# Second cross attention: the value sums of two quads take turns in PSUM banks 2 and 7

## The reference, cut to what matters

```python
def _L1_xattn_ref(query, key, value, mask, Wq, bq, Wk, bk, Wv, bv, Wo, bo):
    ...
    q = proj(query, Wq, bq)
    k = proj(key, Wk, bk)
    v = proj(value, Wv, bv)
    scale = 1.0 / jnp.sqrt(jnp.asarray(DK, q.dtype))
    score = jnp.einsum('bhqd,bhkd->bhqk', q, k) * scale
    m = mask[:, None, :, :]
    score = jnp.where(m == 0, jnp.asarray(-1000000000.0, score.dtype), score)
    p = jax.nn.softmax(score, axis=-1)
    x = jnp.einsum('bhqk,bhkd->bhqd', p, v)
    x = x.transpose(0, 2, 1, 3).reshape(nb, -1, H * DK)
    return x @ Wo.T + bo
...
x = x + _L1_xattn_ref(_layernorm(x, axis=-1), ctx_1024, ctx_1024, mask_Bx1xS2_ik0, ...)
```

## Time and profile before

| | us |
|---|---|
| median of three runs | 2774.32 |
| lowest, highest | 2771.52, 2777.7 |
| the profiled execution's own time | 2772.17 |
| its span (first to last instruction) | 2770.4 |
| TensorE busy over the span | 2404.3 (87%) |
| VectorE, ScalarE, GpSimd busy | 1810.2, 1594.4, 854.7 |
| first and last value matmul of this stage | 2029.5, 2558.9 |

### The profile page before, as it was taken

The page is one execution under the profiler, slowest core; times in us unless marked ns, Lnnn a source line. Parts: engine busy times, 40 slices in busy tenths (PEclk is TensorE's granted clock), DMA queues, the critical chain, the costliest instruction groups (busy, mean ns, idle before and its releaser), DMA issues. The chain is left out here.

```text
span 2770.4 us, 58313 instructions
## 1 busy us (share of the span) xinstructions
PE 2404.3 (87%) x22210; PEld 1544.3 (56%) x22210; DVE 1810.2 (65%) x3862; ACT 1594.4 (58%) x2934; POOL 854.7 (31%) x703
## 2 busy tenths in 40 slices
PE   4389999999999999999679879997799999997786
PEld 2235655555555565555444557774467676775442
DVE  4567677766767776666325379996777777764126
ACT  3245666666665665555613459885457777777113
POOL 2212334333433333222400000001447666656000
PEclk9689999999999999999889979999899999997887
DMA  4312232222322232111152179995643434221302
GB/s 124 105 54 70 69 112 82 68 59 69 93 80 65 63 95 71 34 37 36 53 209 94 41 250 366 364 366 179 207 125 113 128 115 126 84 88 42 122 0 78
DMA packets 256295, 314.14 MB, mean 113 GB/s; under 512 B 71424, under 2 KB 182912, under 8 KB 255120
## 3 DMA queue, kind: packets, MB, share of 16 engines
q1 hardware_dynamic: 252064, 302.28, 34.3%
q10 hardware_dynamic: 3312, 6.03, 0.6%
q0 software_dynamic: 640, 2.10, 0.3%
HBM read 226.56 MB, written 48.10 MB: 99 GB/s over the span
## 5 line engine op out<-in xcount | busy, mean ns | idle before, releaser
L574 POOL TENSOR_TENSOR a_plo<-a_p,a_phi 128x512 bf16<-128x512 f32 x272 | 325.2, 1195 | 790.9 <-ACT a_phi L630 786.1
L766 PE MATMUL ps<-w_hi,a_xhi 128*128 128x512 bf16 x1088 | 419.0, 385 | 0.0
L767 PE MATMUL ps<-w_lo,a_xhi 128*128 128x512 bf16 x1088 | 418.2, 384 | 0.0
L768 PE MATMUL ps<-w_hi,a_xlo 128*128 128x512 bf16 x1088 | 417.3, 384 | 0.0
L1916 POOL TENSOR_TENSOR a_plo<-a_p,a_phi 128x512 bf16<-128x512 f32 x256 | 303.3, 1185 | 182.5 <-ACT a_phi L1953 177.6
L596 ACT ACTIVATE a_kraw<-ps 128x256 f32<-128x256 f32 x272 | 104.2, 383 | 395.3 <-PE ps L768 395.3
L653 DVE TENSOR_TENSOR a_v<-ps,a_v 128x256 bf16<-128x256 f32 x272 | 114.9, 422 | 305.9 <-ACT a_v L598 305.4
L2048 DVE CUSTOM_DVE_ANT_0 a_junk<-ps,a_biasrow 128x512 bf16<-128x512 f32 x256 | 176.1, 688 | 119.4 <-PE ps L2163 118.1
L1948 ACT ACTIVATE a_p<-ps,a_mcol 128x512 f32<-128x512 f32 x256 | 174.9, 683 | 96.7 <-PE ps L2181 90.2
L703 DVE CUSTOM_DVE_ANT_0 a_junk<-ps,a_mrow 128x512 bf16<-128x512 f32 x256 | 174.7, 682 | 19.3 <-PE ps L798 14.6
L626 ACT ACTIVATE a_p<-ps,a_mcol 128x512 f32<-128x512 f32 x256 | 175.4, 685 | 19.9 <-PE ps L818 18.0
(11 more groups left out here) (434 smaller groups left out, 6874.5 us busy)
## 6 DMA issues: line engine op xcount, KB each, us to landing
e_wst<-in_L_ffn_W SPq DMA_DIRECT2D x46, 2048.0 KB, 10.1
a_xn<-in_ctx SPq DMA_DIRECT2D x16, 1024.0 KB, 5.5
a_ks<-a_khi SPq DMA_DIRECT2D x256, 64.0 KB, 2.0
a_ks<-a_klo SPq DMA_DIRECT2D x256, 64.0 KB, 2.0
a_ct<-in_ctxT SPq DMA_DIRECT2D x16, 1024.0 KB, 6.2
a_ks<-k1h_d SPq DMA_DIRECT2D x128, 128.0 KB, 2.5
k1h_d<-a_khi SPq DMA_DIRECT2D x64, 128.0 KB, 2.0
k1l_d<-a_klo SPq DMA_DIRECT2D x64, 128.0 KB, 1.7
```

What stands on the lines that cost most here:

```text
L574: pool.tensor_tensor(p_lo[:, m % 3, :], p32[:, m % 2, :], p_hi[:, m % 3, :], ALU.subtract)\
L766: pe.matmul(out, x_hi[:, c, tile], w_hi[:, c, g, :], start=(c == 0), stop=False)
L767: pe.matmul(out, x_hi[:, c, tile], w_lo[:, c, g, :], start=False, stop=False)
L768: last = pe.matmul(out, x_lo[:, c, tile], w_hi[:, c, g, :], start=False, stop=(c == C - 1))
```

## The change

The bank `PV` = 2 and the bank `ROW` = 7 become one pair. Quad u sums in bank 2 when u is even and in bank 7 when u is odd, and its row of maxima is written into the same bank, four steps before the sums begin. Three waits change. The first value matmul of a quad waits for `row_done` (ScalarE has copied this quad's row out of the bank) instead of `o_evac`. The row's matmul waits for `o_evac` of quad u - 2, the last user of its bank, instead of `row_done` of the quad before. `result` and the copy of the row read the quad's own bank. The order of the instructions on every engine is as before, and so is their number.

```diff
-    PV, KP, VP, ROW = 2, 3, 4, 7
+    KP, VP = 3, 4
...
+    def bank_v(u):
+
+        return (2, 7)[u % 2]
...
-                act.activation(qs[3 * DH1:3 * DH1 + 1, u % 3, :], ps[3 * DH1:3 * DH1 + 1, ROW, :], ACT.Copy)\
+                act.activation(qs[3 * DH1:3 * DH1 + 1, u % 3, :], ps[3 * DH1:3 * DH1 + 1, bank_v(u), :], ACT.Copy)\
...
-                o = ps[:, PV, 0:4 * VW].rearrange("p (h d) -> p h d", d=VW)
+                o = ps[:, bank_v(u), 0:4 * VW].rearrange("p (h d) -> p h d", d=VW)
...
             def maximum_row(u):
                 pe.wait_ge(d_ready, 4 * (u + 1))
-                if u:
-                    pe.wait_ge(row_done, u)
-                pe.matmul(ps[:, ROW, :], onesb[:], Dg[:].rearrange("p h q -> p (h q)"), start=True, stop=True)\
+                if u >= 2:
+                    pe.wait_ge(o_evac, u - 1)
+                pe.matmul(ps[:, bank_v(u), :], onesb[:], Dg[:].rearrange("p h q -> p (h q)"), start=True, stop=True)\
                   .then_inc(row_mm, 1)
...
             def values(m):
                 u, s = divmod(m, NT)
                 if s == 0:
-                    if u:
-                        pe.wait_ge(o_evac, u)
+                    pe.wait_ge(row_done, u + 1)
...
-                    o = ps[:, PV, h * VW:(h + 1) * VW]
+                    o = ps[:, bank_v(u), h * VW:(h + 1) * VW]
```

## The result

The changed kernel takes 2762.48 us (median of six runs, 2758.53 to 2765.37), the kernel before 2772.22 us over its six. The ratio is 0.9967, 95% interval 0.9955 to 0.9979: 5.8 to 12.5 us faster, about 9. The forecast was 2764 us and a gain of 8.7 us. The profiled execution of the changed kernel is the fastest of its six, 2758.53 us with a span of 2756.7, so of the 13.7 us between the two spans not all is the change.

A forecast was written before the change was run, and what follows sets the result against it. TensorE, 94% busy, sets the pace; its largest wait is for VectorE's reciprocal. Boundary gains of 10.4 us less 1.7 for the clock give 8.7 us, forecast 2764 us, 8-in-10 range 2755 to 2770, the forecast's own 2760 to 2767.

The forecast's parts named there:

- The price of the wait: First value matmul of a quad, waiting 14 times for VectorE's reciprocal: 21.4 us in all, the upper end of the gain.
- each late boundary: Boundaries u = 11 to 13, VectorE without a cast left: nothing else comes late, 1.34 us gained each, 4.0 together.
- The new waits and banks at zero: Sums waiting for the row's copy, row matmul for `o_evac` of quad u - 2, row copied from another bank: cost nothing.
- What is late next at an ordinary boundary: u = 2, 3, 6, 7, 10: of 1.66 us, 0.28 lost to values' low part, 0.2 at step 33; 1.2 stays.
- The transfer: Stacked keys read back behind the 1 MB load: slack 1.4 us at u = 3; gain 0 at u = 4, 8.
- its own sign of being wrong: Ordinary boundaries: the forecast is wrong if waits for the maximum or the transfer grow there.
- The other sign: TensorE in the middle: the forecast is wrong if the granted clock falls below 0.98.
- VectorE's chain at u = 1, 5, 9: VectorE's unbroken mask work behind these boundaries keeps its end: gain 0, TensorE's wait for the maximum grows to about 2.3 us.
- The clock: TensorE behind the lengthened wait of 2.6 us at u = 8: one stretch at 1.2 GHz, 1.7 us lost.

The follow-up runs named there:

- the version in pieces: Changed kernel with each 1 MB context load inside the loop issued as four loads of 256 KB, four steps apart: 0.991 to the kernel before, median 2748.84 us.
- the kernel before in pieces: Kernel before, wait kept, with each 1 MB context load issued as four loads of 256 KB: 0.9961 to the kernel before.
- the second profile: Changed kernel, unedited, measured once more beside other runs: 0.996 to the kernel before.
- the loads cut short: Changed kernel with the eleven 1 MB context loads inside the loop cut to an eighth of their columns: 0.9914 to the kernel before.
- sums first: Changed kernel with the value sums first instead of last in a new quad's step 16u + 28: 0.9961 to the kernel before.
- lump moved: Changed kernel with any_kept moved from step 44: its 2.28 us reduction to step 47, three small instructions to step 51: 0.9963 to the kernel before.

## Why the prediction was right

**The price of the wait** held. With the wait back the gain is gone to 0.0003, and 1.34 us at each late boundary, the term with nothing late behind it, measured 1.35; u = 14 gave 0.73 for 0.8.

**The new waits and banks at zero** held: nothing waits for `row_done` at the sums, nor for `o_evac` at the row.

**What is late next at an ordinary boundary**: 0.28 for the values' low part measured 0.30, 0.2 for GpSimd's part of P in step 33 measured 0.39. The net was set at 1.2 and is 1.30 where the transfer is out of the way (u = 10 in the first profile, and every ordinary boundary of the version in pieces against the kernel before in pieces, 33.68 - 32.38), or 0.7 where GpSimd is held up (u = 10 in the second profile).

**The transfer** was the right mechanism, mis-sized. I read the slack of 1.4 us at u = 3 from one profile and carried it to u = 2, 6 and 7. It gave 0.82, 1.03, 0.26, 0.27 for 1.0, 1.2, 1.0, 1.2. Read off the same trace of before, the reads land 0.6, 1.4, 1.1 and 1.7 us ahead of their matmul at u = 2, 3, 6 and 7, so the four slacks could have been told apart. But at u = 7 the reads land 1.35 us later behind the row matmul than before, and at u = 4, where I set the gain to zero, since the transfer "was started before the boundary", 2.2 us later (the wait ends 19.7 and not 17.4 us behind the row matmul), and the quad became 2.15 us longer. The 1 MB load took 8.2 us to land there instead of 5.4 (8.0 in the second profile), and the write of the keys' low part lands 0.7 to 0.8 us behind it each time. Why the load took longer is open. The assumption that failed is that the landing doesn't move. Together these quads gave 4.2 us less than forecast (2.38 for 4.4 at the four, -2.15 for 0). At u = 6 it is not the transfer's doing: with the loads cut short that quad lasts 33.40 us all the same, because VectorE's cast meets GpSimd there. So 0.7 of the 4.2 us belong to a wait that the forecast did not have.

The forecast named its own sign of being wrong: waits for the transfer that grow at the ordinary boundaries. They did, from nothing to 0.87, 0.65, 0.71 and 1.42 us at u = 2, 3, 6 and 7. The other sign, a granted clock below 0.98 in the middle, did not come.

**VectorE's chain at u = 1, 5, 9** was forecast to keep its end; counted from the quad's row matmul it came to an end 1.00 us earlier, three times, and TensorE's wait for the maximum grew to 1.31 and not to 2.3 us. The "gain 0" failed by a contention inside the chain. In the kernel before, the instruction of the mask column (line 2007) starts while GpSimd subtracts:

```profile
2072.11 1.23 DVE L2007 TENSOR_SCALAR a_mcol<-a_kcol,a_some 128x16 f32<-128x16 f32 x1
```

```profile
2072.15 1.16 POOL L1916 TENSOR_TENSOR a_plo<-a_p,a_phi 128x512 bf16<-128x512 f32 x1 [0.79 <-ACT a_phi L1953]
```

In the changed kernel GpSimd comes earlier and is done by then; the same instruction, and the bias row behind it, take their free time, 0.23 and 0.75 us:

```profile
2069.60 0.23 DVE L2011 TENSOR_SCALAR a_mcol<-a_kcol,a_some 128x16 f32<-128x16 f32 x1
2069.74 0.75 DVE L2013 TENSOR_SCALAR a_biasrow<-a_keeprow,a_some 128x2048 bf16<-128x2048 bf16 x1
```

```profile
2067.97 1.16 POOL L1920 TENSOR_TENSOR a_plo<-a_p,a_phi 128x512 bf16<-128x512 f32 x1 [0.80 <-ACT a_phi L1957]
```

The version with the wait put back confirms it from the other side: there the overlap falls on the bias row, and the quad is 36.49 us long, although the mask column takes 0.23:

```profile
2070.73 0.23 DVE L2011 TENSOR_SCALAR a_mcol<-a_kcol,a_some 128x16 f32<-128x16 f32 x1
2070.87 1.66 DVE L2013 TENSOR_SCALAR a_biasrow<-a_keeprow,a_some 128x2048 bf16<-128x2048 bf16 x1
```

```profile
2070.80 1.19 POOL L1920 TENSOR_TENSOR a_plo<-a_p,a_phi 128x512 bf16<-128x512 f32 x1 [0.80 <-ACT a_phi L1957]
```

Before the change VectorE's row ends 0.03 us behind GpSimd's; with the wait put back the bias row ends 0.54 us behind it, somewhat less than the 0.75 us that it takes alone. The Trainium skill (SBUF — State Buffer, section SBUF: two separate sides) describes a port pair that VectorE's two-port modes and GpSimd hold exclusively for a whole instruction; the rows before the change, after it and with the wait put back agree with it.

**The clock** term of 1.7 us didn't show in the first profile and did in the second (1.5 us at u = 8). It is a term with a chance, not a sum: behind waits of 2.4 to 3.8 us at u = 4 and 8 the low stretch came once in four cases (3.84 and 2.48 us in one profile, 3.45 and 2.38 in the other). Behind u = 0 it came after waits of 2.56 (before), 3.26 (sums first) and 3.59 us (lump moved) and not after 2.31 and 2.54 (the changed kernel twice).

So the forecast's 8.7 is right within the measurement, and the price of the wait and the ordinary and late boundaries are right by their mechanism. That the whole sum fits is in part luck: 3.0 us of unforeseen gain at u = 1, 5, 9 and the missing 1.7 us of clock cancel the 4.2 us that five quads gave less.

## What to carry to other kernels

Take a removed wait boundary by boundary: its price is what comes back only where nothing else stands close behind it, here 21.4 us of which 9 came back. Slack of a transfer read from a single profile is no constant, so a large load in front of a small urgent one is worth cutting up before or with such a change. And a lump longer than the period of the double buffer was not hidden by moving it three steps on; cut into pieces of a quarter it vanished from its three quads.

## What the runs showed of the hardware

- VectorE instructions of 0.23 and 0.75 us took 1.23 and 1.66 us when they started within 0.1 us of a GpSimd subtraction of 1.2 us; so which instruction meets which is part of a kernel's time, 3 us in all here.
- Where a VectorE subtraction (0.69 us alone) and a GpSimd one (1.16 us alone) started within 0.02 us of each other, either VectorE took 1.69 and GpSimd 1.16 us, or VectorE 0.69 and GpSimd 1.71; in two executions of the changed kernel it came out differently at u = 10.
- One load of 1 MB against four of 256 KB, same bytes: 0.9961 in the kernel before, and in the changed kernel 0.991 against 0.9967.
- TensorE's clock fell to 1.2 GHz behind a wait of 2.38 us in one execution of the changed kernel and stayed at 2.4 GHz behind waits of 3.84 and 2.48 us in another.
- The stretch between the first two row matmuls lasted 34.67 and 34.91 us in the changed kernel, 37.30 with the lump moved and 37.25 with the sums first, where the same instructions run, and 32.68 with the context in pieces. Behind u = 0 the version in pieces has no wait for the stacked keys, the others have 2.31, 2.54, 3.59 and 3.26 us, the last two with a low clock stretch behind it; so single profiles with the large loads can't tell 2 us there.
